# Squares of the queries: from two GpSimd operations to twelve ScalarE operations

## The chip, the cores and the metric

One core of a Trainium2 chip runs the whole program. The metric is device time in microseconds (us) of one execution. TensorE (PE in the profile) multiplies matrices, VectorE (DVE), ScalarE (ACT) and GpSimd (POOL) work on tiles of 128 partitions, and SyncE (SP) issues the DMAs. Each engine works through its own instructions in order and waits on semaphores.

## The reference

One adaLN transformer block on 4 sequences of 512 tokens and 512 channels, all in float32. A modulation `mod = silu(c) @ wmod` gives shifts, scales and gates. The attention half is a gated delta rule with 6 heads (keys 64 wide, values 128 wide):

```python
h = _layernorm(x) * (1 + ca) + sa
q = short_conv(h @ Wq, conv_wq)      # 4 taps in time, then silu
k = short_conv(h @ Wk, conv_wk)
v = short_conv(h @ Wv, conv_wv)
q = l2norm(q) * dk ** (-0.5)         # needs the sum of q*q over a head's 64 channels
k = l2norm(k)
o = scan: S = S*exp(g); S = S + k (v - kS) beta; o = q S
o = o * rsqrt(mean(o*o) + EPS) * norm_weight * silu(h @ Wg)
x = x + ga * (o @ Wo)
```

The feed-forward half is `silu(h @ w_gate) * (h @ w_up)` times `w_down`, with a norm before it and a gate behind it. The queries' norm is needed late: the kernel leaves `q` unnormalized and puts the sum of its squares, scaled, in place of EPS when it normalizes `o` in the recurrence.

## The kernel before

The program writes one list of steps, `plan`, and then each engine's function walks the list and issues its own part of each step. So the order in `plan` is the order on every engine and in the DMA queue of SyncE (called SPq). There is no scheduler at run time; the semaphores hold what depends on what.

The stages are: norm and modulation of all tokens; projections with the inverse of the delta rule's triangular blocks woven in; a recurrence over 16 units; the feed-forward half. The change lies in the projections.

**Projection steps.** Fifteen weight tiles of 128 columns are projected, each for the four sequences, which makes 60 steps (`slot` 0 to 59). `tile_seq` alternates convolution tiles (0 to 8: queries 0 to 2, values 3 to 8) and gate tiles (9 to 14), until the gates but one are used up. A projection is 12 matmuls of 128x512 (high and low parts of the weights and activations) into one of four PSUM banks; step n issues the projection of step n+1. In a convolution step ScalarE copies the bank, scaled by a tap, into `Y` (`conv_in`), VectorE adds three further taps from the bank (`conv_tap`, L1763), which frees the bank, and in the next step ScalarE applies Silu into one of three buffers `O` (`conv_out`). In a gate step ScalarE applies Silu from the bank into `O` (`gate`), which frees the bank. Each `O` is stored to the scratch `scrU` (`store_u`, L954), and an `O` is used again when its store has landed. At the first step of each tile a weight tile is loaded (`load_w`, L922), copied by ScalarE and split by VectorE (`split_w`).

**Lanes.** Side work is written as generators that give a few pieces to each step: the inverse of blocks (`inverse_1`, then `inverse_2`), the merges behind it, the late modulations, and `q_norms`. `inverse_2` is 31 pairs of a multiplication and an addition on VectorE (L1671), each waiting for the one before, with 93 to 768 elements; convolution steps take one pair, gate steps three operations. It begins at step 17 and ends at step 41. Its result is stored and loaded back (L984, L991), and from step 46 the merges use it (`merge_a`, transposes at L1874, small matmuls).

**The queries' squares.** `q_norms` begins at step 21, when all twelve query pieces (3 tiles by 4 sequences) are stored. Step 21 loads them back into two buffers `QS` of 128x3072; the names `QQ[m][b]` are the twelve pieces of 128x512 in them. GpSimd squares each `QS` in place (L2060). At step 32 TensorE sums the squares over the heads' channels (`q_sum`, matmuls with 32 columns of weights, then a copy by ScalarE), at step 33 it turns the sums (`q_turn`, then eight small copies by ScalarE), and at step 34 GpSimd begins to clear the arrays for the inverse (`clear_p`, memsets at L2070), whose space `QS` shares. `d_cT` counts the loads, 16 for each; its first 16 belong to an earlier load.

**Lines.** Most activations are recorded at L1392, most VectorE operations with two tensors at L1671, and matmuls at L1080, since helpers issue them. L979 issues the twelve loads. L1414 is the table load that `preload_act_table_set` writes; the plan names the set in steps called `table`.

Of the kernel before, what the change touches and what calls it, by code (L numbers as in the profile page):

```python
# [53 lines left out]
def build(nc, x, W1, cw, dtb, alog, nw, Wo, cT, wmod, wg, cst, out):  # L54
    f32, f32r = mybir.dt.float32, mybir.dt.float32r
    ALU, ACT = mybir.AluOpType, mybir.ActivationFunctionType
# [172 lines left out]
    def bank(i):  # L229
        return PSt[:, i, :]  # L230
# [13 lines left out]
    def sem(name):  # L244
        if name not in sems:
            sems[name] = nc.alloc_semaphore(name)
        return sems[name]

    def at_least(tok):
        return sem(tok[0]), tok[1]  # L250
# [3 lines left out]
    def step(kind, **f):  # L254
        f["kind"] = kind
        plan.append(f)
        return f
# [57 lines left out]
    def take():  # L315
        p = pairs["n"] % 2 if last_pair is None else last_pair
        pairs["n"] += 1
        return p, pairs["free"][p]
# [155 lines left out]
        cleared[s] = tick("p_pz")  # L474

    def q_norms():
        step("q_square")
        for _ in range(11):
            yield
        p, free = take()  # L480
        step("q_sum", bank=4 + 2 * p, free=free)
        pfree(p, ("a_k2c", 3))
        yield
        p, free = take()
        step("q_turn", p=p, free=free)
        pfree(p, ("a_k2", 3))
        yield
        clear(3)
        clear(0)
# [416 lines left out]
    def sync(e):  # L906
# [17 lines left out]
        for st in plan:  # L924
# [39 lines left out]
            elif kind == "inv2_load":  # L964
# [4 lines left out]
                blocks = scrA.rearrange("s b t i -> (s b) t i")  # L969
                for i in range(3):  # L970
                    e.dma_start(nAp[:, i, :, :], blocks[128 * i:128 * i + 128]).then_inc(sem("d_nap"), 16)
            elif kind == "q_square":
                e.wait_ge(sem("inv_g"), 16)
                e.wait_ge(sem("k2"), 2)
                for m in range(3):
                    for b in range(4):
                        e.wait_ge(*at_least(stored[(m, b)]))
                        src = scrU.rearrange("(s b) p j t -> b j p s t", b=4)[b, m]
                        e.dma_start(QQ[m][b].rearrange("p (s t) -> p s t", s=4), src).then_inc(sem("d_cT"), 16)  # L979
            elif kind == "inv2_store":  # L980
                e.wait_ge(sem("v_i2a"), 31)
                blocks = scrP.rearrange("s b c t -> (s b) c t")
# [95 lines left out]
    def tensor(e):  # L1078
# [11 lines left out]
        for st in plan:  # L1090
# [67 lines left out]
                t.then_inc(sem("k2"), 1)  # L1158
            elif kind == "q_sum":
                e.wait_ge(*at_least(st["free"]))  # L1160
                e.wait_ge(sem("p_q2"), 2)
                for m in range(3):
                    for g_ in range(4):
                        t = mm(bank(st["bank"])[32 * g_:32 * g_ + 32, :], pick[:, m, :], QQ[m][g_], m == 0, m == 2)
# [225 lines left out]
    def scalar(e):  # L1390
        def act(o, i, f, **kw):
            return e.activation(o, i, f, **kw)  # L1392
# [14 lines left out]
        for st in plan:  # L1407
# [88 lines left out]
            elif kind == "k2":  # L1496
                half = st["half"]
                rows = slice(64 * half, 64 * half + 64)
                e.wait_ge(sem("k2"), half + 1)
                act(kq[rows, :], bank(st["bank"])[rows, :], ACT.Copy).then_inc(sem("a_k2c"), 1)  # L1500
            elif kind == "q_sum":
                e.wait_ge(sem("k2"), 4)
                act(qsum, bank(st["bank"]), ACT.Copy).then_inc(sem("a_k2c"), 1)
# [522 lines left out]
    def gpsimd(e):  # L2026
        done, newest = {}, []

        def in_order():
            if newest:  # L2030
                e.wait_ge(*at_least(newest[0]))

        def signal(ins, name):
            done[name] = done.get(name, 0) + 1
            newest[:] = [(name, done[name])]
            ins.then_inc(sem(name), 1)

        for st in plan:
            kind = st["kind"]
            if kind == "mod":  # L2040
                b, k = st["b"], st["k"]
                e.wait_ge(sem("a_hi"), 4 * b + k + 1)
                in_order()
                signal(e.tensor_tensor(Hlo[:, b, k, :], HF[k][:, :], Hhi[:, b, k, :].bitcast(f32), ALU.subtract), "p_lo")  # L2044
            elif kind == "inv_gm":
                u = st["u"]
                if u == 0:
                    e.wait_ge(sem("v_g"), 1)
                    e.wait_ge(sem("tr"), 16)
                    e.wait_ge(sem("d_cst"), 16)  # L2050
                if u >= 8:
                    e.wait_ge(sem("inv_g"), u - 7)
                sh = [128, H, 64]
                in_order()
                signal(e.tensor_tensor(IG[u % 8][:, :, :], bc(later, 1, sh), bc(g[:, u, :], 2, sh), ALU.mult), "p_ig")  # L2055
            elif kind == "q_square":
                e.wait_ge(sem("d_cT"), 16 + 12 * 16)
                for q_ in QS:
                    in_order()
                    signal(e.tensor_tensor(q_[:, :, :], q_[:, :, :], q_[:, :, :], ALU.mult), "p_q2")  # L2060
            elif kind == "clear_p":
                s = st["s"]
                if s == 1:
                    e.wait_ge(sem("v_i2m"), 31)
                elif s == 2:
                    e.wait_ge(sem("d_pp"), 48)
                else:
                    e.wait_ge(sem("k2"), 5)
                in_order()
                signal(e.memset(P[:, s, :, :], 0.0), "p_pz")  # L2070
            elif kind == "clear_b":
                for tok in st["used"]:
                    e.wait_ge(*at_least(tok))
                in_order()
                signal(e.memset(S[:, :, :], 0.0), "p_zero")
                in_order()
                signal(e.memset(PAT[0][:, :, :], 0.0), "p_zero")
                in_order()
                signal(e.memset(PAT[1][:, :, :], 0.0), "p_zero")
            elif kind == "split_wo":  # L2080
                n = st["n"]
                e.wait_ge(sem("a_wo"), 2 * n + 2)
                in_order()
                signal(e.tensor_tensor(Wol[:, 2 * n:2 * n + 2, :], Wot[:, 2 * n:2 * n + 2, :],
                                Woh[:, 2 * n:2 * n + 2, :].bitcast(f32), ALU.subtract), "p_wo")
            elif kind == "pr_gm":
                u = st["u"]
                if u:
                    e.wait_ge(sem("pr_g"), u)
                else:  # L2090
                    e.wait_ge(*at_least(st["used"]))
                sh = [128, H, 64]
                in_order()
                signal(e.tensor_tensor(GMh[:, :, :], bc(within, 1, sh), bc(ghi[:, u, :].bitcast(f32), 2, sh),
                                       ALU.mult), "p_gm")
                in_order()
                signal(e.tensor_tensor(GMl[:, :, :], bc(within, 1, sh), bc(glo[:, u, :], 2, sh), ALU.mult), "p_gm")
            elif kind == "rec_x":
                u = st["u"]
                pp = place(u)[0]  # L2100
                if before(u):
                    e.wait_ge(sem("v_s"), before(u))
                else:
                    e.wait_ge(sem("p_zero"), 1)
                if u:
                    e.wait_ge(sem("v_s"), u)
                e.wait_ge(sem("v_ex"), 1)
                in_order()
                decay = GC[:, :, u, :]
                signal(e.tensor_tensor(heads(Sg[:, :, :]), heads(S[:, 6 * pp:6 * pp + 6, :]),  # L2110
                                       bc(decay, 3, [128, 2, 3, 128]), ALU.mult), "p_sg")
            elif kind == "po_tr":
                u = st["u"]
                e.wait_ge(sem("a_ozh"), u + 1)
                if u:
                    e.wait_ge(sem("po_wo"), u)
                in_order()
                signal(e.tensor_tensor(OZl[:, :, :], OZ[:, :, :], OZh[:, :, :].bitcast(f32), ALU.subtract), "p_ozl")  # L2118
            elif kind == "po_yg":
                u = st["u"]  # L2120
                e.wait_ge(sem("v_yg"), u + 1)
                e.wait_ge(sem(f"d_xb{u % 2}"), 32 * (u // 2 + 1))
                in_order()
                signal(e.tensor_tensor(YB[u % 2][:, :], YB[u % 2][:, :], XB[u % 2][:, :], ALU.add), "p_x1")  # L2124
            elif kind == "c_split" and st["n"] % 2 == 0:
                n = st["n"]
                hi, lo = norm_out(n)
                e.wait_ge(sem("a_chi"), n + 1)
                in_order()
                signal(e.tensor_tensor(lo, HF2[n % 2][:, :, :], hi.bitcast(f32), ALU.subtract), "p_clo")  # L2130
            elif kind == "out_pre":
                b, s = st["b"], st["s"]
                k = 4 * b + s
                e.wait_ge(sem("v_y"), 16 * (NG - 2) + k + 1)
                if k == 0:
                    e.wait_ge(sem("a_grow"), 6)
                in_order()
                signal(e.tensor_tensor(ya(b, s), ya(b, s), gbB[:, b, :], ALU.mult), "p_out")  # L2138
                e.wait_ge(sem(f"d_xc{b}"), 64)
                in_order()  # L2140
                signal(e.tensor_tensor(ya(b, s), ya(b, s), xo(b, s), ALU.add), "p_out")  # L2141
# [70 lines left out]
```

## Time and profile before

| | us |
|---|---|
| three runs | 1134.74, 1141.09, 1134.94 |
| median | 1134.94 |
| profiled execution, its own time | 1135.77 |
| its span in the trace | 1134.0 |
| TensorE busy | 1058.1 (93%) |
| VectorE busy | 630.7 (56%) |
| ScalarE busy | 372.5 (33%) |
| GpSimd busy | 222.6 (20%) |

Busy times are sums over the whole span, and stages differ: VectorE's 56% is over 90% in the projections and about 30% in the feed-forward half. The granted clock of TensorE is 0.973 of full speed in the mean. Stretches are given in us from the start of the span; the projection steps whose order matters here, 17 to 46, lie between 195 and 291 us.

### The profile page before, as it was taken

The page shows a single profiled execution, that of the slowest core. Times are in us where ns is not written, and L with a number is a line of the kernel's source. Part 1 is how long each engine was busy: PE and PEld are TensorE (multiplying, and loading weights), DVE is VectorE, ACT ScalarE, POOL GpSimd, SP SyncE. Part 2 cuts the span into 40 slices and gives each one's busy share as a digit, 9 for nine tenths or more (in the row PEclk, how much of TensorE's full clock was granted, in tenths as well). Part 3 has the DMA queues.
Part 4 walks back from the last instruction along what each step waited for, and adds up shares of the span by engine and source line. Part 5 has one row for each costly group of instructions (what it writes and reads, how often), then busy time and mean ns, then how long its engine had stood idle before and what let it go on. Part 6 is the DMA issues. An engine that isn't in the chain of part 4 may idle for free.

```text
span 1134.0 us, 18633 instructions
## 1 busy us (share of the span) xinstructions
PE 1058.1 (93%) x7356; PEld 853.7 (75%) x7356; DVE 630.7 (56%) x978; ACT 372.5 (33%) x679; POOL 222.6 (20%) x168
## 2 busy tenths in 40 slices
PE   4898989979788999999877999999999999999998
PEld 2685667758666788888756788788888888888886
DVE  3775454999883677787645334233343334325356
ACT  3575555324444533344245112122121211212110
POOL 0332110221003645455331000000000000004091
PEclk9899999989898999999989999999999999999999
DMA  5502326724717366675612101001010100101223
GB/s 193 190 14 89 88 65 162 213 75 154 144 49 203 70 143 142 157 178 130 207 52 66 56 1 56 1 1 56 1 56 1 33 24 1 56 1 65 72 77 112
DMA packets 153687, 97.88 MB, mean 86 GB/s; under 512 B 93568, under 2 KB 130688, under 8 KB 153472
## 3 DMA queue, kind: packets, MB, share of 16 engines
q1 hardware_dynamic: 153600, 96.68, 31.1%
q8 instruction: 59, 0.97, 0.4%
q14 instruction: 28, 0.23, 0.1%
HBM read 65.19 MB, written 31.46 MB: 85 GB/s over the span
## 4 chain that ended last, share of the span: by engine, by line
PE 79%; DVE 8%; ACT 5%; issue 4%; POOL 1%; DMA 1%; SPq 0%; DVEq 0%; ACTq 0%; POOLq 0%
PE ps L1080 75%; ACT t L1392 5%; DVE t L1671 3%; PE ps L1088 3%; DVE t L1763 2%; PE ps L1280 1%; DVE t L1676 1%; DMA t<-in_x 1%; POOL t L2130 1%; ACT L1414 1%; POOL t L2118 0%; DMA t<-scrU 0%; DVE t L1863 0%; DMA t<-in_wf 0%; DVE t L1681 0%
## 5 line engine op out<-in xcount | busy, mean ns | idle before, releaser
L1080 PE MATMUL ps<-t,t 128*128 128x512 f32 (+6 forms) x6488 | 1000.8, 339 | 56.6 <-DVE t L1763 9.1
L1080 PEld LDWEIGHTS ps<-t,t 128*128 128x128 f32 (+4 forms) x6488 | 793.3, 167 | 240.0 <-issue 48.7
L1671 DVE TENSOR_TENSOR t<-ps,t 128x512 f32<-128x512 f32 (+4 forms) x306 | 208.1, 700 | 255.6 <-PE ps L1080 243.1
L1392 ACT ACTIVATE t<-t 128x512 fp32r<-128x512 f32 (+7 forms) x330 | 184.6, 577 | 341.2 <-DVE t L1671 202.2
L1671 DVE TENSOR_TENSOR t<-t,t 128x512 fp32r<-128x512 f32 (+16 forms) x209 | 169.7, 816 | 114.2 <-ACT t L1392 106.4
L1392 ACT ACTIVATE t<-ps 128x512 f32<-128x512 f32 (+5 forms) x202 | 109.7, 551 | 328.8 <-PE ps L1080 316.0
L2138 POOL TENSOR_TENSOR t<-t,t 128x512 f32<-128x512 f32 x16 | 22.4, 1400 | 404.7 <-DVE t L1671 402.2
L1763 DVE SCALAR_TENSOR_TENSOR t<-ps,t,t 128x511 f32<-128x511 f32 (+2 forms) x108 | 80.3, 747 | 19.8 <-ACT t L1392 17.0
L1088 PE MATMUL ps<-t,t 128*128 128x128 f32 (+1 forms) x388 | 61.0, 292 | 13.3 <-DVE t L1676 9.2
L1392 ACT ACTIVATE t<-ps,t 128x512 f32<-128x512 f32 (+2 forms) x96 | 56.9, 621 | 33.9 <-DVE t L1671 10.3
L1088 PEld LDWEIGHTS ps<-t,t 128*128 128x128 f32 (+1 forms) x388 | 45.7, 149 | 29.6 <-DVE t L1676 13.1
L2118 POOL TENSOR_TENSOR t<-t,t 128x768 fp32r<-128x768 f32 x16 | 29.0, 1813 | 38.8 <-ACT t L1392 38.5
L2124 POOL TENSOR_TENSOR t<-t,t 128x512 f32<-128x512 f32 x16 | 20.5, 1283 | 55.8 <-DVE t L1671 55.6
L2044 POOL TENSOR_TENSOR t<-t,t 128x512 fp32r<-128x512 f32 x16 | 21.2, 1327 | 52.1 <-ACT t L1392 50.3
L2141 POOL TENSOR_TENSOR t<-t,t 128x512 f32<-128x512 f32 x16 | 22.3, 1391 | 40.6 <-DMA t<-scrX 38.6
L1681 DVE BATCH_NORM_STATS2 t<-t 128x6 f32<-128x512 f32 x32 | 22.0, 689 | 13.2 <-DMA t<-in_x 8.4
L1392 ACT ACTIVATE t<-t,t 128x1 f32<-128x1 f32 (+2 forms) x36 | 13.2, 366 | 42.7 <-DVE t L1683 42.6
L1676 DVE TENSOR_SCALAR t<-t,t,t 128x512 f32<-128x512 f32 x32 | 26.4, 824 | 0.6 <-ACT t L1392 0.6
L2060 POOL TENSOR_TENSOR t<-t 128x3072 f32<-128x3072 f32 x2 | 11.2, 5579 | 73.9 <-DMA t<-scrU 73.8
L2055 POOL TENSOR_TENSOR t<-t,t 128x384 f32<-128x384 f32 x16 | 14.0, 873 | 57.5 <-PE ps L1080 38.2
L1751 DVE SCALAR_TENSOR_TENSOR t<-ps,t,t 128x510 f32<-128x510 f32 (+1 forms) x24 | 17.9, 744 | 12.4 <-ACT t L1392 11.8
L2110 POOL TENSOR_TENSOR t<-t,t 128x768 f32<-128x768 f32 x16 | 23.6, 1474 | 2.7 <-POOL t L2124 2.4
(50 smaller groups left out, 241.3 us busy)
## 6 DMA issues: line engine op xcount, KB each, us to landing
scrU<-t SPq DMA_DIRECT2D x60, 256.0 KB, 2.7
t<-in_wf SPq DMA_DIRECT2D x16, 768.0 KB, 4.1
t<-scrU SPq DMA_DIRECT2D x32, 288.0 KB, 4.5
t<-in_wmod SPq DMA_DIRECT2D x6, 1024.0 KB, 5.9
t<-scrU SPq DMA_DIRECT2D x32, 192.0 KB, 3.4
t<-in_W SPq DMA_DIRECT2D x19, 256.0 KB, 2.8
t<-in_x SPq DMA_DIRECT2D x16, 256.0 KB, 3.7
t<-in_x SPq DMA_DIRECT2D x32, 128.0 KB, 2.8
```

The source lines that it names most:

```text
L1080: return e.matmul(o, l, r_, start=start, stop=stop, skip_group_check=True)
L1088: return e.transpose(o, i, idn)
L1392: return e.activation(o, i, f, **kw)
L1671: return e.tensor_tensor(o, a, b, op)
L1676: return e.tensor_scalar(o, a, s1, s2, o1, o2)
L1681: e.bn_stats(st6[:, slot_, :], src).then_inc(sem(name + "bn"), 1)
L1763: e.scalar_tensor_tensor(yy[:, d + 1:SEQ], p_[:, 0:SEQ - d - 1], cwt[:, j, 2 - d:3 - d], yy[:, d + 1:SEQ], ALU.mult, ALU.add).then_inc(sem ...
L2044: signal(e.tensor_tensor(Hlo[:, b, k, :], HF[k][:, :], Hhi[:, b, k, :].bitcast(f32), ALU.subtract), "p_lo")
L2110: signal(e.tensor_tensor(heads(Sg[:, :, :]), heads(S[:, 6 * pp:6 * pp + 6, :]), bc(decay, 3, [128, 2, 3, 128]), ALU.mult), "p_sg")
L2118: signal(e.tensor_tensor(OZl[:, :, :], OZ[:, :, :], OZh[:, :, :].bitcast(f32), ALU.subtract), "p_ozl")
L2138: signal(e.tensor_tensor(ya(b, s), ya(b, s), gbB[:, b, :], ALU.mult), "p_out")
L2141: signal(e.tensor_tensor(ya(b, s), ya(b, s), xo(b, s), ALU.add), "p_out")
```

## The change

The single step `q_square` becomes two kinds. `q_load` (steps 21, 22 and 23) issues four loads each, one query tile of the four sequences. `q_square` (steps 28, 29 and 30) has ScalarE square four pieces of 128x512 each, in place, once all twelve loads have landed. GpSimd's two instructions of 128x3072 are gone. `q_sum` stays at step 32 and waits for twelve squares by ScalarE in place of two by GpSimd.

```diff
     def q_norms():
-        step("q_square")
-        for _ in range(11):
+        for m in range(3):
+            step("q_load", m=m)
             yield
+        for _ in range(4):
+            yield
+        for m in range(3):
+            step("q_square", m=m)
+            yield
+        yield
         p, free = take()
         step("q_sum", bank=4 + 2 * p, free=free)
...
-            elif kind == "q_square":
-                e.wait_ge(sem("inv_g"), 16)
-                e.wait_ge(sem("k2"), 2)
-                for m in range(3):
-                    for b in range(4):
-                        e.wait_ge(*at_least(stored[(m, b)]))
-                        src = scrU.rearrange("(s b) p j t -> b j p s t", b=4)[b, m]
-                        e.dma_start(QQ[m][b].rearrange("p (s t) -> p s t", s=4), src).then_inc(sem("d_cT"), 16)
+            elif kind == "q_load":
+                m = st["m"]
+                if m == 0:
+                    e.wait_ge(sem("inv_g"), 16)
+                    e.wait_ge(sem("k2"), 2)
+                for b in range(4):
+                    e.wait_ge(*at_least(stored[(m, b)]))
+                    src = scrU.rearrange("(s b) p j t -> b j p s t", b=4)[b, m]
+                    e.dma_start(QQ[m][b].rearrange("p (s t) -> p s t", s=4), src).then_inc(sem("d_cT"), 16)
...
             elif kind == "q_sum":
                 e.wait_ge(*at_least(st["free"]))
-                e.wait_ge(sem("p_q2"), 2)
+                e.wait_ge(sem("a_q2"), 12)
...
+            elif kind == "q_square":
+                e.wait_ge(sem("d_cT"), 16 + 12 * 16)
+                for q_ in QQ[st["m"]]:
+                    act(q_, q_, ACT.Square).then_inc(sem("a_q2"), 1)
...
-            elif kind == "q_square":
-                e.wait_ge(sem("d_cT"), 16 + 12 * 16)
-                for q_ in QS:
-                    in_order()
-                    signal(e.tensor_tensor(q_[:, :, :], q_[:, :, :], q_[:, :, :], ALU.mult), "p_q2")
```

## Rows read from the trace of the kernel before

**Rows 1.** The page, costliest groups: busy, mean ns; idle before, releaser.

```profile
L2060 POOL TENSOR_TENSOR t<-t 128x3072 f32<-128x3072 f32 x2 | 11.2, 5579 | 73.9 <-DMA t<-scrU 73.8
```

**Rows 2.** Timeline of GpSimd: start us, duration us, instruction, idle before.

```profile
218.98 5.31 POOL L2060 TENSOR_TENSOR t<-t 128x3072 f32<-128x3072 f32 x1 [73.78 <-DMA t<-scrU]
224.37 5.85 POOL L2060 TENSOR_TENSOR t<-t 128x3072 f32<-128x3072 f32 x1
251.24 5.46 POOL L2070 MEMSET t<- 128x3072 f32 x2 [21.02 <-PE ps L1080]
```

**Rows 3.** Chain of waits from 180 to 340: start us, us, what.

```profile
221.01 4.05 DVE t L1671
...
225.09 5.89 DVE t L1671
...
286.81 3.61 issue
```

**Rows 4.** Timeline of VectorE.

```profile
218.70 2.31 DVE L1763 SCALAR_TENSOR_TENSOR t<-ps,t,t 128x511 f32<-128x511 f32 x3
220.93 10.06 DVE L1671 TENSOR_TENSOR t<-t,t 128x720 f32<-128x720 f32 x2
...
247.80 2.31 DVE L1763 SCALAR_TENSOR_TENSOR t<-ps,t,t 128x511 f32<-128x511 f32 x3
250.02 1.84 DVE L1671 TENSOR_TENSOR t<-t,t 128x720 f32<-128x720 f32 x2
...
255.71 2.31 DVE L1763 SCALAR_TENSOR_TENSOR t<-ps,t,t 128x511 f32<-128x511 f32 x3
...
290.35 1.57 DVE L1874 STREAM_TRANSPOSE t<-t 32x192 f32<-32x192 f32 x4 [0.90 <-DMA t<-scrP]
```

**Rows 5.** Timeline of ScalarE.

```profile
220.03 0.63 ACT L1392 ACTIVATE t<-t 128x512 f32<-128x512 f32 x1 [5.31 <-DMA scrU<-t]
...
221.35 1.14 ACT L1392 ACTIVATE t<-t 128x512 f32<-128x512 f32 x2
233.30 0.63 ACT L1392 ACTIVATE t<-t 128x512 f32<-128x512 f32 x1 [10.81 <-DVE t L1763]
233.84 1.07 ACT L1392 ACTIVATE t<-ps 128x512 f32<-128x512 f32 x2
239.06 0.60 ACT L1392 ACTIVATE t<-ps 128x512 f32<-128x512 f32 x1 [4.15 <-DMA scrU<-t]
...
252.09 0.69 ACT L1392 ACTIVATE t<-ps,t 128x512 f32<-128x512 f32 x1
```

**Rows 6.** Timeline of TensorE.

```profile
233.26 53.55 PE L1080 MATMUL ps<-t,t 128*128 128x512 f32 x260 [9.14 <-DVE t L1763]
```

**Rows 7.** A window: length, busy PE, PEld, DVE, ACT, POOL, clock, DMA, GB/s.

```profile
235.00:237.00 2.00, 2.00 (x6) 1.52 (x6) 1.97 (x4) 0.00 (x0) 0.00 (x0) 0.50 0.16 53
```

**Rows 8.** All waits of VectorE from 195 to 291: us, times, longest.

```profile
DVE t L1671 <- DMA t<-scrA: 3.0, 1, 3.0
DVE t L1874 <- DMA t<-scrP: 0.9, 1, 0.9
```

**Rows 9.** A window of 10 us, columns as above.

```profile
200.00:210.00 10.00, 10.00 (x46) 8.29 (x45) 9.59 (x16) 4.01 (x7) 0.00 (x0) 1.00 0.75 208
```

**Rows 10.** Timeline of the DMA queue of SyncE: start us, us of issuing.

```profile
204.30 10.03 SPq L979 DMA_DIRECT2D t<-scrU  x12
```

**Rows 11.** ScalarE by form, 89 to 97, then its timeline behind the load at 117.

```profile
L1392 ACT ACTIVATE t<-t 128x1536 f32<-128x1536 f32 x3 | 4.5, 1485 | 0.0
L1414 ACT ACT_TABLE_LOAD x1 | 1.3, 1283 | 0.0
...
119.94 0.60 ACT L1392 ACTIVATE t<-t 128x96 f32<-128x96 f32 x2 [1.38 <-DVE t L1798]
```

**Rows 12.** TensorE by form, 242 to 243, then 243 to 244.

```profile
L1080 PE MATMUL ps<-t,t 128*32 128x512 f32 x8 | 1.1, 604 | 0.0
...
L1080 PE MATMUL ps<-t,t 128*32 128x512 f32 x24 | 2.8, 596 | 0.0
```

## The prediction

> **What bounds the kernel now.** I began with the page. GpSimd is busy a fifth of the span, yet its squaring line is remarkable: two instructions of 5.6 us each, after a long wait for their loads [rows 1]. The question is what else happens in those 11 us. I asked for GpSimd's own order [rows 2] and for the chain of waits over the projection stage [rows 3]. There the chain runs over VectorE, where a multiplication and an addition of the inverse take 4.05 and 5.89 us; TensorE comes back only at 233.26 [rows 6]. The same form, 720 elements, takes 1.84 us for a multiplication and an addition together at 250.02 [rows 4]. What fits is not size but time. The first multiplication starts at 220.93, inside GpSimd's first square (218.98 + 5.31 = 224.29), and ends 0.76 us behind it, at 225.06. The second starts at 225.09, inside the second square (224.37 + 5.85 = 230.22), and ends 0.76 us behind that, at 230.98. Each stood still for the whole rest of a GpSimd instruction. The three convolution taps at 218.70, which read PSUM and one SBUF tile, took their usual 2.31 us beside the same square; ScalarE too took its usual 0.63 us at 220.03 beside it [rows 5]. GpSimd's memsets stopped nobody: the first pair spans 251.24 to 256.7 [rows 2], and the taps at 255.71 took 2.31 us as ever [rows 4]; they read one SBUF tile, so that row alone is weak, but the pair from 250.02 to 251.86, too, overlaps the memset's start and took its 1.84 us. So it is a VectorE instruction with two SBUF inputs against a GpSimd instruction that reads SBUF.
>
> Does that time count? TensorE idles 9.14 us, waiting for VectorE [rows 6], and its granted clock stands at 0.50, the 1.2 GHz level, until 237, behind that idle time [rows 7]. But VectorE is the engine with no slack. From 195 to 291 its only waits are 3.0 us for the blocks of the inverse, at the start, and 0.9 us at the end [rows 8]; it is busy for 9.59 of the 10 us from 200 [rows 9], and what is missing are gaps of 0.03 us between instructions. TensorE is full as well, but when both come to the first merge TensorE waits 3.61 us there while VectorE still works on the taps ahead of it [rows 3, 4]. So VectorE, with its 62 dependent inverse steps woven among the taps, sets the end of this stretch.
>
> **What the change removes.** GpSimd's two squares go, and with them 10.06 - 1.84 = 8.22 us of VectorE standing still [rows 4]. Everything VectorE does from 231 on moves forward by that. The merge's first transpose at 290.35 waited 0.9 us for the inverse to be loaded back [rows 4]; that path of DMAs starts with VectorE's last inverse step, so it moves forward with it. Behind the merge the kernel is the same work. Gain: 8.2 us.
>
> GpSimd's later instructions lose a predecessor, nothing more: the first memset comes 21 us after the squares [rows 2]. Their cover is not needed.
>
> **What it adds.** Twelve squares of 128x512 on ScalarE, in place. No row has one alone. The Silu and Square activations of 128x1536 take 1.485 us [rows 11], 0.50 us per 512 columns; a single 128x512 from SBUF takes 0.63 us, and two in a row 1.14 us, a pitch of 0.52 [rows 5]. Twelve at 0.52 and three starts are 6.6 us; at 0.63 each, the upper end, 7.6. I take 6.6, since the squares stand four in a row. They fall into the first three steps of a gate tile (steps 28 to 30), where ScalarE did three instructions between 233.30 and 234.91 and then waited 4.15 us for an output buffer's store [rows 5].
>
> I lay them into the new order, all times less 8.2. The convolution output starts at 225.1, the first gate ends at 226.3, four squares to 228.4, gate to 229.0, four squares to 231.1, gate (its buffer is free at 239.06 - 8.2 = 230.9) to 231.7, four squares to about 234.0. The last gate, the weight split and the next evacuation end at about 236. VectorE wants that at 247.80 - 8.2 = 239.6 [rows 4]: hidden with 3 us over. TensorE wants the second gate's bank for its third projection from the tap that it waits for now: 225.0 + 2 x 2.61 = 230.3 (2.61 us is 12 of the 46 matmuls in 10 us [rows 9]; 225.0 is 233.26 less 8.2), and has it at 229.0.
>
> The sum over heads on TensorE now waits for the twelfth square. In the trace it begins near 242.6: 8 of its matmuls fall into 242 to 243 and all 24 records touch 243 to 244 [rows 12]. Less 8.2 that is 234.4, against squares ready at 234.0 (235.0 at the upper price). TensorE itself would be free at 232.9, so it idles 1 to 2 us. That costs nothing unless it reaches VectorE. What is queued behind: the next projection, the turn of the sums, ScalarE's eight small copies and then its evacuation at 252.09, done at 252.78; VectorE uses that at 255.71 [rows 4, 5]. The sum may thus come 2.9 us later than its shifted place before VectorE notices. Cost: 0, bounds 0 and 0.
>
> TensorE does not get away free of waiting either: it runs dry at 233.26 - 9.14 = 224.1 and the taps that it waits for now end at 225.0, so 0.9 us of its 9.14 stay. It is off the path, like the clock that it lost.
>
> **The loads.** Today one block of twelve issues occupies the DMA queue from 204.30 to 214.33, and the stores of two gates stand behind it [rows 10]; ScalarE waits 5.31 us for one until 220.03 [rows 5]. In three parts of four (3.3 us each, 0.84 us an issue) the first goes at 204.3 as before, the others behind the stores of the next two gates. Those stores leave up to 7 us earlier, which is worth nothing, since VectorE never waited for them; the last load has two issues more ahead of it and leaves 1.7 us later. Its data landed at 218.98 [rows 2], so now near 220.7, and ScalarE wants it at 226.3: 5.6 us of cover. If that cover were gone, each us past 226.3 + 2.9 + 0.4 = 229.6 would cost one.
>
> **Sum.** The profiled execution took 1135.77 us, span 1134.0, which is 0.83 above the median of 1134.94. 1135.77 - 8.2 = 1127.6; at the median, 1126.7.
>
> **A rule weighed.** From 89 to 97 ScalarE runs one table load and three activations of 128x1536, which by the plan are Silu, Silu and Square [rows 11]; no load stands between the kinds. So I charge none. The Trainium skill, "ScalarE: Activation LUTs", section "What ACT_TABLE_LOAD costs", puts every switch to a different set at about 2.66 us including a drain, and would charge that whenever Silu gates alternate with a function outside their set. By that rule five switches would stand before the last square, about 13 us, and the sum would be a loss; it bears on the last rival.
>
> **Rivals.**
> *TensorE's loss is the price.* If TensorE were the limiter behind 233, what returns is its idle time and its slow clock: 9.14 - 0.9, plus half of the 3.74 us at 0.50 from 233.26 to 237 [rows 6, 7] = 10.1 us, time 1124.8; with the remaining 0.9 us gone too, 11.0 us and 1123.9. For it: TensorE is full from 233 to 286. Against: it arrives 3.61 us early at the merge, the dip included. The Trainium skill's "TensorE: Matmul & The Clock Gate", Part 1, says that an idle engine drops to half rate until it has been busy again; the trace agrees [rows 7], but the rule prices only TensorE. 12%.
> *Part of the gain is given back by ScalarE.* The loads land late, or squares hold its in-order queue. Loads landing 12 us later, at 232: squares end at 239.7, 5.3 us past the sum's place, 2.4 past the slack: gain 5.8, time 1129.1. With 2 us more, 1131. For: three parts behind two stores. Against: 5.6 us of cover. 10%.
> *No change.* The stall is taken up elsewhere before the merge, 1134.9. For: several engines are nearly full. Against: VectorE's row of waits is empty. 8%.
> *Slower.* Table switches around Square. The place is steps 28 to 30; the price, a load of 1.283 us and the 1.38 us of idling behind the one at 117, before the activation at 119.94, is 2.65 us at most [rows 11], since that idle time may have had another cause. Five of them put the last square at 234.0 + 13.3 = 247.3, the sum 12.9 late, 2.9 of it slack: VectorE idles 10.0 us, 1.8 more than was gained, time 1136.7. It decides from 11.1 us of lateness on. Rows 11 speak against it, strongly. 4%, worse prices included.
> The forecast has the rest, 66%.
>
> **Numbers.** 1% is 11.3 us, about what a measurement of this kernel tells from no change: below 1123.6 or above 1146.3. The forecast by itself spans 1125 to 1129 (noise of the runs shown, and the clock dips of later stages, which need not fall alike). The range of 1122.5 to 1131.0 takes in the first two rivals and leaves out no change and slower, with the forecast's tails about 18%. Faster by over 1%: half of the first rival and the low tail, 12%. Slower by over 1%: only a multiple of the last rival's price, 3%. Within 1%: 85%.
>
> **What would show it.** Right: the 720-element pair near 221 takes about 1.85 us; TensorE's idle there is 1 us or so, with the clock at 1.00; twelve activations lie in three groups with a pitch near 0.5 us; VectorE has no new wait up to the merge; the merge begins near 282 instead of 290.35. Wrong: a VectorE wait for ScalarE or TensorE near 247, a table load between 225 and 236, ScalarE waiting for a load at its first square, or a merge that begins at 290 all the same.

## The result, and the profile after

The changed kernel takes 1128.2 us in the median of six runs (1126.64 to 1132.12), the kernel before beside it 1135.83 us in six: ratio 0.9931, 95% interval 0.9908 to 0.9955, or 7.6 us less. The forecast was 1126.7 us, in a range of 1122.5 to 1131.0. One of all the runs in this study was slow: 1335.34 us at a mean granted clock of 0.751, in the kernel with one projection more (below), where the other nine had 0.970 to 0.979; its ratio leaves that run out. The profiled execution took 1130.92 us with a span of 1129.1, which is 2.7 us above its median, while that of before lay 0.8 above the median shown then. So the two spans differ by 4.9 us only, and a reader who stops there would look for 3 us that are not lost. I therefore measure the stretch that the prediction is about, from VectorE's 180-element pair (step 18) to the first merge transpose (step 46): 290.35 - 197.72 = 92.63 us before. Its start, and the first operations on VectorE behind the stall, in the kernel before:

```profile
197.72 0.72 DVE L1671 TENSOR_TENSOR t<-t,t 128x180 f32<-128x180 f32 x2
...
233.12 14.76 DVE L1671 TENSOR_TENSOR t<-t,t 128x741 f32<-128x741 f32 x16
```

Here is VectorE's timeline after (start us, duration us), as [rows 4]:

```profile
199.73 0.72 DVE L1682 TENSOR_TENSOR t<-t,t 128x180 f32<-128x180 f32 x2
...
222.92 1.84 DVE L1682 TENSOR_TENSOR t<-t,t 128x720 f32<-128x720 f32 x2
...
226.91 14.77 DVE L1682 TENSOR_TENSOR t<-t,t 128x741 f32<-128x741 f32 x16
...
271.02 0.54 DVE L1682 TENSOR_TENSOR t<-t,t 128x93 f32<-128x93 f32 x2
...
284.07 1.56 DVE L1885 STREAM_TRANSPOSE t<-t 32x192 f32<-32x192 f32 x4 [0.78 <-DMA t<-scrP]
```

The pair of 10.06 us takes 1.84 us, the pair's usual time, and 284.07 - 199.73 = 84.34 us: the stretch is 8.29 us shorter. Of that, 8.22 us lie ahead of the group of 16 (233.12 - 197.72 = 35.40 against 226.91 - 199.73 = 27.18), and from there to the merge VectorE takes the same time, 57.23 and 57.16 us. The stretch began 2.0 us later than before, where both kernels issue the same work, and what follows it took 845.0 us against 843.65. Those two differences, 3.4 us, hide two fifths of the gain in this one pair of profiles. Both vary by more than that among the profiles of this study (below), so I don't read them as effects of the change.

All waits of VectorE from 195 to 291 (total us, times, longest), as [rows 8]:

```profile
DVE t L1682 <- DMA t<-scrA: 3.5, 1, 3.5
DVE t L1874 <- PE ps L1087: 1.0, 1, 1.0
DVE t L1885 <- DMA t<-scrP: 0.8, 1, 0.8
```

No wait has taken the place of the stall: the first row lies ahead of the stretch, the last is the old 0.9 us, and the middle one lies behind the merge's start. TensorE's timeline, as [rows 6]:

```profile
223.06 3.01 PE L1087 MATMUL ps<-t,t 128*128 128x512 f32 x12 [0.43 <-DVE t L1774]
227.05 8.46 PE L1087 MATMUL ps<-t,t 128*128 128x512 f32 x36 [0.97 <-DVE t L1774]
235.86 19.05 PE L1087 MATMUL ps<-t,t 128*32 128x512 f32 x116 [0.35 <-ACT t L1399]
255.75 24.78 PE L1087 MATMUL ps<-t,t 128*128 128x512 f32 x108 [0.84 <-DVE t L1774]
284.14 1.49 PE L1087 MATMUL ps<-t,t 32*32 32x32 f32 x48 [3.61 <-issue]
```

One wait of 9.14 us has become three small ones for the taps (0.43, 0.97 and 0.84 us). At the third row TensorE begins the sum of squares, 0.35 us late, and it waited for ScalarE: the last square. In front of the merge it stands idle for 3.61 us, just as before. Its clock holds at 1.00, the 2.4 GHz level, behind its wait of 0.97 us, where [rows 7] has 0.50 behind the wait of 9.14 us (busy us and instructions of PE, PEld, DVE, ACT, POOL, then the clock):

```profile
227.00:229.00 2.00, 1.95 (x8) 1.61 (x9) 1.97 (x3) 1.91 (x4) 0.00 (x0) 1.00 0.03 8
```

ScalarE's timeline, as [rows 5], has the twelve squares in three groups, each behind a gate; the DMA queue's shows the three parts of the loads with a gate's store between them:

```profile
228.10 2.18 ACT L1399 ACTIVATE t<-t 128x512 f32<-128x512 f32 x4
230.19 0.58 ACT L1399 ACTIVATE t<-ps 128x512 f32<-128x512 f32 x1
230.66 2.19 ACT L1399 ACTIVATE t<-t 128x512 f32<-128x512 f32 x4
...
233.53 2.18 ACT L1399 ACTIVATE t<-t 128x512 f32<-128x512 f32 x4
...
245.39 0.69 ACT L1399 ACTIVATE t<-ps,t 128x512 f32<-128x512 f32 x1
```

```profile
206.30 2.85 SPq L986 DMA_DIRECT2D t<-scrU  x4
...
209.74 3.82 SPq L986 DMA_DIRECT2D t<-scrU  x4
...
214.31 3.47 SPq L986 DMA_DIRECT2D t<-scrU  x4
```

### The profile page after: what moved, and what is told of

Read it like the earlier page. It is cut to its first block, busy times and chain, and to the rows that moved or that the text cites. A ratio compares the mean times of both kernels' runs of the same rounds, so it can differ in the third digit from the quotient of the medians.

```text
span 1129.1 us, 18642 instructions
## 1 busy us (share of the span) xinstructions
PE 1060.3 (94%) x7356; PEld 853.6 (76%) x7356; DVE 623.2 (55%) x978; ACT 378.3 (34%) x691; POOL 212.0 (19%) x166
## 4 chain that ended last, share of the span: by engine, by line
PE 74%; DVE 11%; ACT 5%; issue 4%; DMA 3%; SPq 2%; POOL 1%; DVEq 0%; ACTq 0%; POOLq 0%
PE ps L1087 70%; DVE t L1682 5%; ACT t L1399 5%; DVE t L1774 3%; PE ps L1095 3%; DVE t L1687 1%; PE ps L1287 1%; SPq L967 1%; DMA t<-in_x 1%; POOL t L2136 1%; DMA t<-scrA 1%; SPq L1024 1%; ACT L1421 1%; DMA t<-scrU 0%; DVE t L1874 0%
## 5 line engine op out<-in xcount | busy, mean ns | idle before, releaser
L1399 ACT ACTIVATE t<-t 128x512 fp32r<-128x512 f32 (+7 forms) x342 | 191.3, 579 | 338.5 <-DVE t L1682 202.9
L1682 DVE TENSOR_TENSOR t<-t,t 128x512 fp32r<-128x512 f32 (+16 forms) x209 | 162.1, 780 | 115.2 <-ACT t L1399 106.8
L2076 POOL MEMSET t<- 128x3072 f32 x4 | 10.7, 2668 | 124.4 <-PE ps L1087 97.8
```

The costliest lines, as they stand in the source:

```text
L1682: return e.tensor_tensor(o, a, b, op)
```

## The experiments

Theory A is the prediction's: VectorE stands still while GpSimd reads SBUF (the on-chip memory that holds the tiles), and VectorE sets the pace. For each kernel I give the stretch from its own profile, and the ratio of its runs to the kernel before on the same chip. The stretch is what decides, since the ratios have intervals of some 0.3% (3 us) to either side and can't tell most of these kernels apart. Each stretch comes from one profile. How well it repeats is seen from the five kernels below that leave VectorE's work as the change has it (changed, changed once more, squares alone, memsets later, one projection more): 84.19 to 84.49 us.

| kernel | stretch, us | ratio (95% interval) |
|---|---|---|
| before | 92.63 | |
| changed | 84.34 | 0.9931 (0.9908 to 0.9955) |
| loads alone | 92.36 | 0.9988 (0.9965 to 1.0011) |
| squares alone | 84.49 | 0.9915 (0.9880 to 0.9951) |
| GpSimd reads later | 94.35 | 0.9998 (0.9972 to 1.0023) |
| GpSimd memsets later | 84.19 | 0.9894 (0.9851 to 0.9936) |
| one projection more on TensorE | 84.43 | 0.9938 (0.9906 to 0.9970) |
| VectorE 2.9 us more | 87.37 | 0.9944 (0.9912 to 0.9977) |
| GpSimd squares in pieces | 90.44 | 0.9973 (0.9944 to 1.0003) |
| seven splits beside taps | 87.72 | 0.9946 (0.9924 to 0.9969) |
| three splits beside taps | 82.57 | 0.9879 (0.9852 to 0.9906) |
| three splits at once | 85.48 | 0.9932 (0.9903 to 0.9961) |
| changed, once more | 84.49 | 0.9932 (0.9908 to 0.9956) |

**The loads alone.** GpSimd squares as before.

```diff
     def q_norms():
-        step("q_square")
-        for _ in range(11):
+        for m in range(3):
+            step("q_load", m=m)
+            if m == 2:
+                step("q_square")
             yield
+        for _ in range(8):
+            yield
```

> GpSimd squares as before, only the loads issued in three parts. I measure the stretch from VectorE's 180-element pair to the first merge transpose: 92.63 us before, 84.34 after. Theory A (VectorE stands still while GpSimd reads): stretch 92 to 93 us, the two 720-element operations together again near 10 us (or two neighbours of them, if the loads land some other time), ratio 1.000. Rival B (the loads and the stores queued behind them gave the gain): stretch near 84.3, ratio 0.993.

VectorE, then GpSimd:

```profile
196.22 0.72 DVE L1676 TENSOR_TENSOR t<-t,t 128x180 f32<-128x180 f32 x2
...
219.43 6.83 DVE L1676 TENSOR_TENSOR t<-t,t 128x720 f32<-128x720 f32 x2
226.18 2.31 DVE L1768 SCALAR_TENSOR_TENSOR t<-ps,t,t 128x511 f32<-128x511 f32 x3
228.40 17.67 DVE L1676 TENSOR_TENSOR t<-t,t 128x741 f32<-128x741 f32 x16
...
288.58 1.56 DVE L1879 STREAM_TRANSPOSE t<-t 32x192 f32<-32x192 f32 x4 [0.91 <-DMA t<-scrP]
```

```profile
219.64 11.78 POOL L2065 TENSOR_TENSOR t<-t 128x3072 f32<-128x3072 f32 x2 [75.76 <-DMA t<-scrU]
```

The loads gain nothing. The stall has shifted a little against the steps, and is instructive for it: the pair loses 6.83 - 1.84 = 4.99 us to the first square, the group of 16 loses 17.67 - 14.77 = 2.90 us to the second, and between them the taps run at 2.31 us beside a square that is under way. 7.9 us in all, close to what the stretch says (92.36 - 84.34 = 8.02).

**The squares alone.** The twelve loads in one block.

```diff
         for m in range(3):
             step("q_load", m=m)
-            yield
-        for _ in range(4):
+        for _ in range(7):
             yield
```

> ScalarE squares in three steps, the twelve loads in one block as before. Theory A: stretch 84.3 us, ratio 0.993. Rival B: stretch near 92.6, ratio 1.000.

84.49 us: the whole gain comes from the squares. (Its ratio's interval, 0.5% to 1.2% less, holds the 0.7% of the changed kernel.)

**GpSimd reads again, later.** In the changed kernel, ahead of the first memset of step 34; the values are dead by then.

```diff
                 else:
                     e.wait_ge(sem("k2"), 5)
+                if s == 3:
+                    for q_ in QS:
+                        in_order()
+                        signal(e.tensor_tensor(q_[:, :, :], q_[:, :, :], q_[:, :, :], ALU.mult), "p_q2")
                 in_order()
```

> The changed kernel, and two GpSimd multiplications of 128x3072 more, ten steps later, ahead of the first memset (they square values that nobody reads any more). Theory A: the inverse's multiplication and addition near 244 us wait 5 us each, stretch 84.3 + 10 = 94.4 us, ratio about 1.001 to the kernel before; the taps between them keep 2.31 us a group. Rival C (TensorE's idle time and its clock are the price, not VectorE's): the stretch grows by TensorE's idle time plus its slow clock, over 11 us. Rival D (only the place near 221 was sensitive): nothing changes, 0.993.

VectorE, then GpSimd, then TensorE:

```profile
197.61 0.72 DVE L1682 TENSOR_TENSOR t<-t,t 128x180 f32<-128x180 f32 x2
...
241.72 11.81 DVE L1682 TENSOR_TENSOR t<-t,t 128x720 f32<-128x720 f32 x2
...
291.96 1.56 DVE L1885 STREAM_TRANSPOSE t<-t 32x192 f32<-32x192 f32 x4 [0.83 <-DMA t<-scrP]
```

```profile
241.53 11.24 POOL L2078 TENSOR_TENSOR t<-t 128x3072 f32<-128x3072 f32 x2 [97.72 <-PE ps L1087]
```

```profile
255.81 7.60 PE L1087 MATMUL ps<-t,t 128*128 128x512 f32 x24 [8.71 <-DVE t L1774]
```

The stall is back at another place, 11.81 - 1.84 = 9.97 us, and the stretch is 10.0 us longer. TensorE's idle time is 8.71 us, and behind it the granted clock is 0.50 from 256 to 258 and 0.56 in the mean from 258 to 260, so the 1.2 GHz level held for nearly 4 us of TensorE's work and cost it some 2 us (an estimate from these two windows). With its later waits shorter by 0.6 (0.20 us for 0.84), TensorE's own loss is about 10 us too. So this kernel shows that the stall follows GpSimd's reading, but not whose loss counts; for that, TensorE and VectorE have to be loaded one at a time, as below.

**GpSimd memsets at that place.** The same with `signal(e.memset(q_[:, :, :], 0.0), "p_q2")` in the loop.

> The same place as the kernel with two more GpSimd multiplications, but two more GpSimd memsets of 128x3072 (2.7 us each), which read nothing. Theory A: VectorE's pairs keep 1.84 and 1.79 us, stretch 84.3 us, ratio 0.993. Rival (any GpSimd instruction on SBUF blocks VectorE): about 5 us more.

GpSimd, then VectorE:

```profile
244.03 5.41 POOL L2078 MEMSET t<- 128x3072 f32 x2 [97.52 <-PE ps L1087]
```

```profile
200.15 0.72 DVE L1682 TENSOR_TENSOR t<-t,t 128x180 f32<-128x180 f32 x2
...
244.27 1.84 DVE L1682 TENSOR_TENSOR t<-t,t 128x720 f32<-128x720 f32 x2
248.25 1.79 DVE L1682 TENSOR_TENSOR t<-t,t 128x693 f32<-128x693 f32 x2
...
284.34 1.56 DVE L1885 STREAM_TRANSPOSE t<-t 32x192 f32<-32x192 f32 x4 [0.62 <-DMA t<-scrP]
```

Nothing is blocked, though GpSimd writes SBUF all through both pairs. The Trainium skill, "SBUF — State Buffer", section "Who interferes with whom", says so: a VectorE instruction with two SBUF inputs contends with a GpSimd instruction that reads SBUF, not with one that only writes. The last two kernels agree, 9.97 us against 0. (They differ in the operation as well as in the reading, a multiplication against a memset; a GpSimd multiplication that reads no SBUF was not run.)

**TensorE or VectorE?** Two kernels add work to one engine each. First a projection done twice:

```diff
+    TWICE = [(13, 2)]
...
-                for k in range(4):
+                for k in [*range(4)] * (2 if (st["wn"], b) in TWICE else 1):
                     e.wait_ge(sem("p_lo"), 4 * b + k + 1)
```

> The changed kernel with one projection more: the twelve matmuls that step 33 issues for step 34 are done twice (2.6 us of TensorE, around 240 us), everything else as changed. Stretch as defined: VectorE's 180-element pair to the first merge transpose, 84.3 us in the changed kernel. Theory A (VectorE sets the pace, TensorE has room): stretch 84.2 to 84.6 us, TensorE's small waits for the taps near 255 shrink, and its 3.6 us in front of the merge stay or shrink. Rival C (TensorE sets the pace): stretch 1.8 to 2.6 us longer.

Then three multiplications of the inverse more (their result is the one that is computed anyway):

```diff
+                    for n in range(3 if i == 14 else 0):
+                        tt(t_, bc(Pp[:, :, j, j:32], 2, sh), bc(nAp[:, :, j, 0:j], 3, sh), ALU.mult).then_inc(sem("v_dup"), 1)
+                        e.wait_ge(sem("v_dup"), n + 1)
                     tt(t_, bc(Pp[:, :, j, j:32], 2, sh), bc(nAp[:, :, j, 0:j], 3, sh), ALU.mult).then_inc(sem("v_i2m"), 1)
```

> The changed kernel with three more VectorE multiplications of 128x756 (0.97 us each, the inverse's own multiplication of step 28 repeated, near 230 us), everything else as changed. Theory A: stretch 84.3 + 2.9 = 87.2 us, and TensorE has a wait of up to 3 us for taps, which is all that it loses. Rival C: the stretch grows by less than 1 us, since TensorE's banks carry it over.

TensorE of the first kernel, then VectorE of the second:

```profile
237.47 45.97 PE L1089 MATMUL ps<-t,t 128*32 128x512 f32 x236 [0.32 <-ACT t L1401]
285.83 0.95 PE L1089 MATMUL ps<-t,t 32*32 32x32 f32 x48 [2.39 <-issue]
```

```profile
227.82 17.75 DVE L1682 TENSOR_TENSOR t<-t,t 128x741 f32<-128x741 f32 x19
```

From the sum of squares to the merge, TensorE's busy time grows by 2.1 us (45.97 for 19.05 + 24.78; the expectation's 2.6 us is the length of a projection when it runs without a gap), and the stretch by 0.1 us. The rest went into TensorE's wait of 0.84 us near 255, which is gone, and into the wait in front of the merge, 2.39 for 3.61 us. 2.98 us more of VectorE (17.75 - 14.77) cost 87.37 - 84.34 = 3.03 us. The rival by which TensorE's idle time and clock were the price is refuted. The kernel before says the same of the clock: TensorE ran at 0.50 until 237 there and at 1.00 after the change, and yet VectorE took 57.23 and 57.16 us from the group of 16 to the merge.

**GpSimd's squares in twelve pieces.** The kernel before with `for q_ in QQ[0] + QQ[1] + QQ[2]` on GpSimd, and the sum waiting for twelve.

> The kernel before, with GpSimd squaring the same values in twelve pieces of 128x512 (about 1.0 to 1.3 us each) in place of two of 128x3072. Theory A: each inverse step waits for the rest of one piece, and two pieces fit under each group of taps, so VectorE loses less than 8.2 us but still 3 to 7: stretch 87 to 91 us, ratio 0.995 to 0.999. Rival (the loss is the sum of GpSimd's reading time, however cut): stretch 92 us or more.

GpSimd, then VectorE:

```profile
220.85 17.66 POOL L2060 TENSOR_TENSOR t<-t 128x512 f32<-128x512 f32 x12 [73.95 <-DMA t<-scrU]
```

```profile
227.60 20.19 DVE L1671 TENSOR_TENSOR t<-t,t 128x741 f32<-128x741 f32 x16
```

GpSimd's own time grows from 11.24 to 17.66 us, and yet VectorE loses less: 90.44 - 84.34 = 6.1 us. Most of it, 20.19 - 14.77 = 5.4 us, falls on the inverse steps of the gate tile, where no taps give cover.

**Going on from there.** If taps are free cover, GpSimd can take work from VectorE there. A weight tile's low part costs VectorE 0.68 us. Seven of them move to GpSimd; the number behind a tile is the inverse step whose end starts it, since VectorE's taps come next. The first cut below is on VectorE, the second on GpSimd:

```diff
+    GP_SPLITS = {9: 0, 11: 9, 13: 19, 15: 29, 16: 0, 17: 0, 18: 0}
...
+                if j in GP_SPLITS:
+                    continue
...
+            if kind == "split_w" and st["j"] in GP_SPLITS:
...
+                e.wait_ge(sem("a_whi"), j + 1)
+                e.wait_ge(sem("v_wlo"), j)
+                if GP_SPLITS[j]:
+                    e.wait_ge(sem("v_i2a"), GP_SPLITS[j])
+                in_order()
+                e.tensor_tensor(WL[h][:, :, :], Wraw[j % 2][:, :, :], WH[h][:, :, :].bitcast(f32),
+                                ALU.subtract).then_inc(sem("v_wlo"), 1)
```

> A step beyond the change: the low part of seven weight tiles (VectorE 0.68 us each) is computed by GpSimd, each started at the moment when VectorE begins its three taps, which read PSUM and one SBUF tile. Theory A: GpSimd's 1.3 us lie under 2.31 us of taps and block nothing; three of the tiles lie on VectorE's path, stretch 84.3 - 2.1 = 82.2 us, ratio about 0.991. Rival (any work handed to GpSimd beside a full VectorE costs it as much as it saves): stretch 84.3 or more.

VectorE, then GpSimd, then the DMA queue:

```profile
197.86 0.72 DVE L1684 TENSOR_TENSOR t<-t,t 128x180 f32<-128x180 f32 x2
...
267.35 0.54 DVE L1684 TENSOR_TENSOR t<-t,t 128x93 f32<-128x93 f32 x2
...
285.58 1.56 DVE L1891 STREAM_TRANSPOSE t<-t 32x192 f32<-32x192 f32 x4 [6.57 <-DMA t<-scrP]
```

```profile
274.50 2.67 POOL L2094 MEMSET t<- 128x3072 f32 x1 [4.17 <-DMA scrP<-t]
277.34 1.26 POOL L2066 TENSOR_TENSOR t<-t,t 128x512 fp32r<-128x512 f32 x1 [0.17 <-POOL t L2094]
```

```profile
278.63 0.33 SPq L928 DMA_DIRECT2D t<-in_W  x1
...
279.55 6.89 SPq L998 DMA_DIRECT2D t<-scrP  x10
```

My expectation of 82.2 us failed: 87.72. Up to the last inverse step theory A held: 267.35 - 197.86 = 69.49 us, against 71.29 in the changed kernel (its row at 271.02), 1.8 us gained. Then VectorE waits 6.57 us for the inverse. The split of step 44 stood on GpSimd behind a memset that itself waits for the inverse's store; the next weight load waits for that split; and the inverse's loads back stand behind the weight load in one queue. I had looked at what the moved instruction blocks on VectorE and not at what it is queued behind.

**Three splits**, 11, 13 and 15 alone, in the same way:

> The changed kernel, and the low parts of three weight tiles only (those split at steps 24, 32 and 40) computed by GpSimd, each started when VectorE begins its taps. In the run with seven such splits VectorE gained 1.8 us up to its last inverse step, and lost more behind it, because the split of step 44 stood behind a memset on GpSimd and a weight load stood behind it in the DMA queue, ahead of the inverse's loads; that split stays on VectorE here. Theory A: stretch 84.3 - 1.8 = 82.5 us, and the wait for the inverse's loads at the merge is 0.8 us again. Rival: some other wait at the merge takes the gain, 84.3.

**The same three**, each started as soon as its input is there (`{11: 0, 13: 0, 15: 0}`):

> The same three splits on GpSimd, but started as soon as ScalarE has the high part, which is in the middle of VectorE's inverse steps. Theory A: each costs an inverse step up to 1.3 us of standing still and saves 0.6: stretch 84.3 to 86.4 us, not 82.5. Rival (GpSimd's work is free where it is short): 82.5 us.

VectorE's timeline of the first kernel, and then the same group of inverse steps in the second:

```profile
199.24 0.72 DVE L1684 TENSOR_TENSOR t<-t,t 128x180 f32<-128x180 f32 x2
...
202.10 9.80 DVE L1684 TENSOR_TENSOR t<-t,t 128x261 f32<-128x261 f32 x15
...
281.81 1.57 DVE L1891 STREAM_TRANSPOSE t<-t 32x192 f32<-32x192 f32 x4 [0.83 <-DMA t<-scrP]
```

```profile
200.16 10.77 DVE L1684 TENSOR_TENSOR t<-t,t 128x261 f32<-128x261 f32 x15
```

GpSimd's timeline of the first kernel, one of its splits beside taps, and then of the second, two splits in the middle of inverse steps:

```profile
240.26 1.28 POOL L2066 TENSOR_TENSOR t<-t,t 128x512 fp32r<-128x512 f32 x1 [26.47 <-DVE t L1684]
```

```profile
207.98 1.45 POOL L2066 TENSOR_TENSOR t<-t,t 128x512 fp32r<-128x512 f32 x1 [64.20 <-ACT t L1399]
...
261.82 1.56 POOL L2066 TENSOR_TENSOR t<-t,t 128x512 fp32r<-128x512 f32 x1 [14.75 <-ACT t L1399]
```

Beside taps the stretch is 82.57 us, 1.8 less than the changed kernel and as expected. The wait at the merge is 0.83 us, so the long wait of the seven splits came with the four that are left out. Started at once, the three give 85.48 us, 2.9 more: each of VectorE's three groups of 15 is 0.97 us longer (10.77 for 9.80, 15.13 for 14.16, 10.76 for 9.79). The same three instructions save 1.8 us or cost 1.1, and only their starting moment differs. The kernel with three splits beside taps has the lowest median here: 1124.81 us in six runs, ratio 0.9879 (0.9852 to 0.9906), against 1131.84 us in eleven runs and 0.9932 (0.9908 to 0.9956) for the changed kernel beside it:

> The changed kernel once more, on the chip of the two other kernels. Stretch 84.3 us; the rest of the span varies between profiles by 1 to 3 us on either side of the stretch. Ratio 0.993 to the kernel before, and 1.8 us above the kernel with three splits beside taps.

That kernel repeated its ratio and its stretch, 84.49 us. The medians of the two differ by 7 us and the stretches by 1.9; the intervals of the ratios just miss each other. My expectation of 1.8 us for the medians failed with that. 1.9 us are explained, the other 5 are not, and I don't claim them: in the two profiles 3.8 us of them lie behind the merge and 1.4 ahead of the stretch. Outside the stretch the spans of the profiles vary in all kernels: it begins between 196.2 and 201.3 us, and what follows takes 840.7 to 846.7 us, with no order by kernel that I can see. What sets that was not tested. For the same reason the ratio of the kernel with memsets, 0.9894, is no gain over the changed one.

## Why the prediction was right

The forecast was 8.2 us, the stretch gave 8.29, the runs 7.6. The stretch holds the mechanism; that the medians agree too is as good as their noise, since what lies outside the stretch varies by several us from profile to profile. Step by step:

- *The stall is GpSimd's reading.* Shown: it follows the two instructions to another place (9.97 us), memsets there do nothing, and without any of them it is gone.
- *VectorE sets the pace, TensorE's loss is off the path.* Shown by 3.03 us for 2.98 on the one and 0.1 for 2.1 on the other. The rival with 12% is refuted. What spoke against it in the trace of before, the 3.61 us in front of the merge [rows 3], stood at 3.61 again, with a loss of 9.14 us ahead of it and without.
- *Squares on ScalarE.* Forecast 6.6 us in all, at a pitch of 0.52. Each group of four takes 2.18 or 2.19 us, 6.55 in all. The last ended at 233.53 + 2.18 = 235.71; the forecast's 234.0 with the stretch's 2.0 us of later start is 236.0. The evacuation of step 34 was done at 246.08, and VectorE used it at 249.52: slack of 3.4 us, forecast 2.9. ScalarE's rows from 220 to 250 hold no table load.
- *The sum's wait.* Forecast 1 to 2 us of idle TensorE, measured 0.35. TensorE started its three projections at 227.05, as forecast (225.0 + 2.0), but they took 8.46 us and not 3 x 2.61 = 7.83, and the squares ended 0.3 us earlier than forecast. The forecast also has the sum's old place wrong: the two lines of [rows 12] are those of the windows 243 to 244 and 244 to 246, not 242 to 243 and 243 to 244. In the kernel before the sum begins near 243.5, so its shifted place is 235.3 and not 234.4. After the change it began at 235.86, or 233.9 without the later start of 2.0 us: ahead of that place. The cost of 0 stands, with about 1 us more of room than the forecast gave it; the prices of the two rivals that make the sum late are too high by as much.
- *TensorE's remaining wait.* Forecast 0.9 us, measured 0.97 at that place, and 0.43 and 0.84 for taps at two others which the forecast did not name. That a TensorE which no longer lags behind runs into VectorE's taps more often fits VectorE as the pace. I had treated the one wait of before as the only place.
- *The loads.* The last issue came at 217.78, forecast 216.0 + 2.0; ScalarE never waited for a load. Issuing them in parts is worth nothing: 92.36 us alone, and 84.49 without it against 84.34 with it.
- *Given back, no change, slower*: neither ScalarE nor the merge's loads took the gain. The mechanism of the seven splits, a queue that holds the inverse's loads, shows what such a rival would have looked like; the change does not touch that queue there.

The profiled execution after, taken by its span, shows a gain of 4.9 us only. A prediction made against one profile's span must be tested on the stretch that it argues about.

## What to carry to other kernels

Ask of every GpSimd instruction that reads SBUF which VectorE instructions with two SBUF inputs lie beside it: here those stood still until it ended, and their rows showed that as busy time, not as a wait, so that only the comparison with the same form elsewhere (10.06 against 1.84 us) gave it away. Give such work to ScalarE if it has idle time, or start it where VectorE reads one of its two tiles from PSUM, the banks that TensorE writes; three short instructions started there saved 1.8 us and started at once cost 1.1. When an instruction moves to another engine, look at both queues: what it will stand behind, and what waits for its signal in the DMA queue.

## What the runs showed of the hardware

The two engines seem to take turns. In [rows 2] the second square starts at 224.37, while VectorE's released multiplication runs to 225.06, and takes 5.85 us where the first took 5.31. I read this so: GpSimd waited for VectorE in its turn, and yet it got ahead of the addition that followed. That would be why both halves of the pair stalled and not the first alone; it is argued from the durations, and those of GpSimd are rough in a profile. The small ones fit: a split takes 1.26 to 1.30 us beside taps and 1.37 to 1.56 in the middle of inverse steps. With pieces the turns are many: twelve instructions of 128x512 cost VectorE 6.1 us, where two of 128x3072 cost 8.3, though GpSimd itself was busy longer.
